# A six-layer local-attention stack on one Trainium2 core: who writes the attention mask and the rotation tables, and in which order gates, mix and projections stand

## The reference

```python
def local_attention(q, k, v):          # windows of 32 queries look at 64 keys
    ...
    mask = (it < jb) | (it > jb + w) | (jb == -1)
    sim = jnp.einsum('bhwie,bhwje->bhwij', bq, bk2) * QK_SCALE
    sim = jnp.where(mask, -jnp.finfo(sim.dtype).max, sim)
    attn = jax.nn.softmax(sim, -1)
    return jnp.einsum('bhwij,bhwje->bhwie', attn, bv2).reshape(b, h, n, d)
def attn_layer(x, Wqkv, qs, ksc, Wo):
    q, k, v = ...                      # x @ Wqkv, split in heads
    q, k = l2norm(q) * qs, l2norm(k) * ksc
    q = q * cos * scale + rotate_half(q) * sin * scale
    k = k * cos * inv + rotate_half(k) * sin * inv
    return local_attention(q, k, v) @ Wo   # heads joined
def ffn_layer(x, g, bln, W1, b1, W2, b2):
    a, gate = jnp.split((layernorm(x) * g + bln) @ W1 + b1, 2, -1)
    return a * jax.nn.gelu(gate, approximate=False) @ W2 + b2
for i in range(6):
    x = attn_layer(shift_tokens(x), ...) + x
    x = ffn_layer(shift_tokens(x), ...) + x
```

## Time and profile before

| | us |
|---|---|
| median of 3 runs | 1973.81 |
| lowest and highest | 1972.79, 1976.53 |
| profiled execution, its own time | 1982.47 |
| its span, first to last instruction | 1980.7 |
| stack, first projection to last down product | 568.7 to 1513.1 |

### The profile page before, as it was taken

One profiled execution on the slowest core, in us unless ns is written; L12 is line 12 of the kernel. 1 busy time (PEld: TensorE's weight loads), 2 busy tenths in 40 slices (PEclk: granted clock), 3 DMA queues, 4 the chain that ended last, 5 costly groups with the idle time before them and its releaser, 6 DMA issues.

```text
span 1980.7 us, 42335 instructions
## 1 busy us (share of the span) xinstructions
PE 1643.8 (83%) x17341; PEld 1101.0 (56%) x17341; DVE 1277.5 (64%) x2385; ACT 923.0 (47%) x1681; POOL 750.6 (38%) x1058
## 2 busy tenths in 40 slices
PE   3005576998778899899998999899987999999999
PEld 1002354675545556656655656656654677667576
DVE  6847674213857787878877878788863666666311
ACT  1034132332334556556655656556553666666232
POOL 0000030100256666656765756656740333334000
PEclk6556797899879999999999999999998999999999
DMA  3000002010043433423423433342321000000111
GB/s 106 20 4 0 3 1 61 22 33 14 1 129 95 132 82 91 128 73 100 134 77 88 126 97 98 97 105 84 89 54 43 1 1 2 1 1 1 33 33 32
DMA packets 73806, 113.38 MB, mean 57 GB/s; under 512 B 16086, under 2 KB 36156, under 8 KB 73582
## 3 DMA queue, kind: packets, MB, share of 16 engines
q1 hardware_dynamic: 72798, 110.43, 20.1%
q10 hardware_dynamic: 816, 0.24, 0.1%
HBM read 83.98 MB, written 27.50 MB: 56 GB/s over the span
## 4 chain that ended last, share of the span: by engine, by line
PE 60%; DVE 27%; ACT 6%; issue 5%; DMA 1%; DVEq 1%; POOL 0%; ACTq 0%; POOLq 0%; SPq 0%
PE PS L1387 8%; PE PS L1115 6%; PE PS L1106 6%; PE PS L1576 4%; PE PS L2066 4%; PE PS L2020 3%; PE PS L2045 3%; PE PS L1624 3%; PE PS L1490 3%; DVE st_t L1430 2%; DVE st_ss L1435 2%; DVE st_r L1422 2%; PE PS L1516 2%; DVE al_hist L459 1%; PE PS L1600 1%
## 5 line engine op out<-in xcount | busy, mean ns | idle before, releaser
L1463 POOL TENSOR_TENSOR st_r<-st_r,st_t 128x512 f32<-128x512 f32 x192 | 243.6, 1274 | 261.2 <-DVE st_t L1430 261.2
L1387 PE MATMUL PS<-st_wqkv,st_xs 128*128 128x512 f32 x576 | 304.1, 612 | 16.3 <-DVE st_xs L1637 9.3
L2151 POOL TENSOR_SCALAR la_p<-la_p,la_rden 128x589 f32<-128x589 f32 x64 | 112.8, 1763 | 246.0 <-DVE la_rden L2170 246.0
L1478 POOL TENSOR_TENSOR st_r<-st_r,st_gy 128x512 f32<-128x512 f32 x192 | 196.6, 1056 | 3.8
L1422 DVE TENSOR_TENSOR st_r<-PS,st_rot 128x512 f32<-128x512 f32 x192 | 129.9, 677 | 90.3 <-ACT st_sqh L1406 89.9
L2164 DVE TENSOR_REDUCE la_nmx<-PS 128x1 f32<-128x589 f32 x128 | 92.7, 766 | 91.8 <-PE PS L2028 91.8
L2126 ACT ACTIVATE la_p<-PS,la_nmx 128x589 f32<-128x589 f32 x128 | 95.1, 748 | 106.5 <-DVE la_nmx L2164 106.5
L1174 ACT ACTIVATE m_h<-PS 128x512 f32<-128x512 f32 x128 | 76.4, 598 | 142.3 <-PE PS L1106 142.3
L1406 ACT ACTIVATE st_sqh<-PS 128x512 f32<-128x512 f32 x192 | 114.3, 595 | 58.9 <-PE PS L1387 58.9
L1199 DVE SCALAR_TENSOR_TENSOR m_y<-PS,m_g,m_y 128x128 f32<-128x128 f32 x112 | 31.5, 344 | 161.0 <-PE PS L1115 161.0
L1430 DVE TENSOR_TENSOR st_t<-PS,st_rot 128x512 f32<-128x512 f32 x192 | 130.6, 680 | 0.0
(11 more groups left out here) (312 smaller groups left out, 3491.0 us busy)
## 6 DMA issues: line engine op xcount, KB each, us to landing
st_v_out<-st_v SPq DMA_DIRECT2D x48, 512.0 KB, 2.6
st_vv<-st_v_out SPq DMA_DIRECT2D x96, 256.0 KB, 3.8
st_vv<-st_v_out SPq DMA_DIRECT2D x96, 192.0 KB, 4.7
st_wqkv<-in_st_wqkv SPq DMA_DIRECT2D x18, 512.0 KB, 5.8
m_w<-in_m_w SPq DMA_DIRECT2D x32, 256.0 KB, 3.1
st_vv<-st_v_out SPq DMA_DIRECT2D x72, 64.0 KB, 1.9
st_wo<-in_st_wo SPq DMA_DIRECT2D x6, 512.0 KB
st_w<-in_st_w SPq DMA_DIRECT2D x6, 341.0 KB
```

The source lines that it names most:

```text
L1387: pe.matmul(PS[:, 2 + m % 2, :], self.xs[:, b, P * t:P * t + P], self.wqkv[:, l % 2, k, 512 * half:512 * half + 512], start=True, stop=Tru ...
L1463: pool.tensor_tensor(r, r, self.t2[:, c % 2, :], ALU.add).then_inc(self.added, 1)
L1478: pool.tensor_tensor(r, r, y[:, 8 * c:8 * c + 8].unsqueeze(2).broadcast_to([P, 8, D2]), ALU.mult)\
L2151: pool.tensor_scalar(self.p[:, v % 2, 0, :], self.p[:, v % 2, 0, :], self.rden[:, v % 4, 0:1], None, ALU.mult).then_inc(self.scaled0, 1)
```

## The change

Five things change, all in `Stack`.

1. The mask is written into banks 0 and 1 by a ScalarE copy (`act_mask`), at the end of the step before the one that uses it, once `on_ready` tells that the banks are free. The identity matmuls and `identb` are gone. The scores add onto what ScalarE wrote; for this two matmuls at T = -1 write both banks once, and `pe_mix` starts an accumulation only with the first of the four heads that share a bank and column group.
2. The rotation tables are made on GpSimd (`pool_tables`), Q's behind the second addition of the layer's last tile and K's behind its scalings, one signal each.
3. In `pe`, projection 0 of T+2 and the first half of the output transposes stand ahead of the scores; where T+2 begins a new batch half (t = 2), projection 0 stays behind the scores. At t = 1 the mix stands ahead of up product 1.
4. In `dve`, at t = 1 gate 0 stands ahead of the denominator and gate 1 behind the output; at t = 2 the down sum and the shift stand ahead of the guess, which is a function of its own.
5. In `act`, the table load for Exp stands behind the mask and not ahead of the K evacuations.

```diff
@@ dve_proj, dve_tables
-            if c == 0 and T % (B * self.TILES) == 0:
-                self.dve_tables(dve, l)
+            if c % 2 == 0 and T % (B * self.TILES) == 0:
+                dve.wait_ge(self.rot_ready, 2 * l + 1 + k)
...
+        def pool_tables(self, pool, l, k):
+            pool.wait_ge(self.qks_in, l * 16 + 16)
+            for j in range(2):
+                ins = pool.tensor_tensor(self.rot[:, k, j, :, :], self.base[:, k, j, :, :],
+                                         self.qks[:, k, j, :].unsqueeze(1).broadcast_to([P, 4, D2]), ALU.mult)
             ins.then_inc(self.rot_ready, 1)
@@ pool_proj
                 pool.tensor_tensor(r, r, self.t2[:, c % 2, :], ALU.add).then_inc(self.added, 1)
+                if c == 1 and following:
+                    self.pool_tables(pool, following, 0)
...
+            if following:
+                self.pool_tables(pool, following, 1)
@@ pe_scores
-            if T > 0:
-                pe.wait_ge(self.on_ready, T)
-            for e in range(2):
-                pe.matmul(PS[:, e, :], self.identb[:, :],
-                          self.wmask[:, min(t, 1), :].unsqueeze(1).broadcast_to([P, 8, 2 * WIN]),
-                          start=True, stop=False, skip_group_check=True)
+            pe.wait_ge(self.masked, T + 2)
...
+        def act_mask(self, act, T):
+            t = T % self.TILES
+            if T == 0:
+                act.wait_ge(self.c_in, 32)
+                act.wait_ge(self.masked, 1)
+            else:
+                act.wait_ge(self.on_ready, T)
+            act.activation(PS[:, 0:2, :].rearrange("p e (c k) -> p (e c) k", c=8),
+                           self.wmask[:, min(t, 1), :].unsqueeze(1).broadcast_to([P, 16, 2 * WIN]), ACT.Copy)\
+               .then_inc(self.masked, 1)
@@ pe_mix
-                                   self.vv[:, 4 * (T % 2) + w, :, D2 * c:D2 * c + D2], start=True, stop=True,
+                                   self.vv[:, 4 * (T % 2) + w, :, D2 * c:D2 * c + D2], start=(c % 4 == 0), stop=(c % 4 == 3),
@@ pe
+                if T == -1:
+                    for e in range(2):
+                        mm = pe.matmul(PS[:, e, :], const("centre"), self.xs[:, 0, :], start=True, stop=True)
+                    mm.then_inc(self.masked, 1)
+                if past:
+                    self.pe_turn_o(pe, T - 1, 0)
+                fresh = lead and (T + 2) % self.TILES == 0
+                if lead and not fresh:
+                    self.pe_proj(pe, T + 2, 0)
                 if here:
                     self.pe_scores(pe, T)
-                if past:
-                    self.pe_turn_o(pe, T - 1, 0)
-                if lead:
+                if fresh:
                     self.pe_proj(pe, T + 2, 0)
```

More of the change, by code:

```diff
@@ L1829, in act @@
                     self.act_gelu(act, end_of, 2)
-                if norm_of is not None or end_of is not None:
-                    self.act_table(act, ACT.Exp)
                 if turn:
@@ L1888, in pool @@
                 pool.wait_ge(self.set_up, k + 1)
+            pool.wait_ge(self.c_in, 32)
+            for k in range(2):
+                self.pool_tables(pool, 0, k)
             for T in range(self.N):
```

53 lines of the change are left out of this document (25 added, 28 removed).

## The result

| | us |
|---|---|
| changed kernel, median of 4 runs | 1955.32 |
| lowest and highest | 1947.39, 1962.84 |
| kernel before, 4 runs beside it | 1975.17 (1972.79 to 1984.96) |
| ratio, 95% interval | 0.9874 (0.9839 to 0.9908) |
| profiled execution after, its own time | 1947.39 (before 1982.47) |

The time is inside the range and the change is faster, its interval clear of 1, but by 19.9 us between these medians (25 us by the ratio) where 40.1 was forecast; the forecast ratio of 0.980 lies outside the interval. The two profiled executions differ by 35.1 us: that of before stands above its median, that of after is the fastest of its four.

A forecast was written before the change was run, and what follows sets the result against it. TensorE, 83% busy, was taken as the main bound, with a 14.75 us VectorE loop from t = 2 to 3. Gains of 27.0, 1.5, 2.4 and 9.5 less 0.3 made 40.1 us: 1973.8 to 1933.7, range 1917 to 1958.

The forecast's parts named there:

- the gate rival: At t = 1 up product 2 gets no earlier than today, 10 x 1.53 + 1.5 lost: 1950 us; chance 0.17.
- the pauses for instructions: TensorE's waits for late instructions in the stack: left at zero, 12 us either way; off by more, chance 0.07.
- Part 1, the mask: ScalarE mask, 1.06 us: t=3, 0 and 1 gain 0.53, wait 0.46 anew, about 0.07 left; wait hidden at t=2.
- Part 2, t = 1: From VectorE's first rotation product C, down product starts at C+11.0, not C+12.53: gain 1.53 us, new wait 0.9.
- Part 3, t = 2: Down sum ahead of the guess: projection 0 starts 4.6 us behind the down product, against 5.79; gain 1.17.
- Part 4: VectorE's first rotation products: t=2 to 3 stays 14.75 us; t=3 to 0 goes from 15.14 to 14.9, gain 0.2.
- Part 5, the tables: Rotation tables on GpSimd, 0.5 to 1.06 us per product, hidden; saves 9.5 us over 5 layers.
- The sum: Stack gains 27.0, 1.5, 2.4 and tables 9.5, less 0.3 for priming matmuls: 40.1 us in total.
- The steps named as unlucky: Steps whose score block starts at place 160 to 220 of 256 TensorE instructions, expected to stall; about as many as now.
- More than twelve stalls for issue: Sign that the forecast is wrong: over twelve TensorE waits for late instructions in the profile after; nine were counted before.
- The clock rival: New TensorE waits of 0.46 and 0.9 us lower its clock in 44 steps, 75 us come back: 2009; chance 0.07.

The follow-up runs named there:

- the unchanged copy: The changed kernel as it is, run again beside three kernels with added waits: 1958.96 us, ratio to before 0.9887.
- 149 waits each: Satisfied TensorE waits, 149 at the stack's start plus some per group, added to the changed kernel (1944.17 us) and the kernel before (1971.60 us).
- waits placed anew: Satisfied TensorE waits moved to an early pause (138, 135) and re-chosen per group, in the changed kernel (1927.51 us) and the kernel before (1955.34 us).

## Why the prediction was right or wrong

**Direction and range were right, the forecast time was 21.6 us too low** (1933.7 against 1955.32). Of that, 1.1 us is in the steps, 7.6 in the pauses and 11.5 between the stack of the profiles and the medians; 1.4 is the median of the kernel before, which a fourth run raised from 1973.8 to 1975.17. The range owes its upper end to the gate rival with more stalls. The gate rival did not come true, so that 1955 lies inside is in part luck. The step that failed is the pauses for instructions, left at zero. Of the chain of numbers:

- *Part 1, the mask.* Its row is 1.02 us (1080.75) where 1.06 was taken. The Trainium skill (ScalarE: Activation LUTs, "Step-by-step: what each stage is for") says that ScalarE writes PSUM faster than SBUF; the trace agrees weakly, 1.02 us against 1.05 for ScalarE's exp of the same size into SBUF (1070.73), but function and source type differ too, so the port alone was not measured. The wait for it is 0.40 us at t = 1, forecast 0.46. At t = 3 and t = 0 there is none. There the step failed: it forgot that projection 0, moved ahead of the scores, has a releaser of its own, VectorE's second product (0.40 at 1081.06). That wait stands ahead of the projection, and behind the projection the mask is ready. The size is the same, so the step came out. The worth of the part was put too low, though. Undone alone the mask costs 0.91 us a group, of which 0.43 at t = 2, where the text spoke only of the new wait, as hidden.
- *Part 2, t = 1.* From C = 1052.20 the down product starts at C+11.05 (1063.25); forecast C+11.0. The new wait is 0.63, forecast 0.9, and gone is the one before up product 1 (1055.82). Undone: 1.56 us; forecast 1.53.
- *Part 3, t = 2.* Projection 0 starts 4.52 us behind the down product (1063.25 to 1067.77); forecast 4.6. But the 1.17 us were credited to the sum's order alone. Undoing this costs 0.65 to 0.79 us and the mask's matmuls 0.43 at t = 2, together 1.1 to 1.2: the sum was right, its parts were not.
- *Part 4.* VectorE's first products stand 14.80 us apart from t = 2 to 3 (1227.05 to 1241.85; forecast 14.75) and 14.95 from t = 3 to 0 (forecast 14.9).
- *Part 5, the tables.* 0.73 us each on GpSimd, inside 0.5 to 1.06, hidden as forecast: steps with tables take 15.82, the others 15.76, where they took 17.23 and 15.54. With the 0.2 us of the step behind that is 1.84 us in each of 5 layers, 9.2 in all; forecast 9.5. Undone in the new order the tables cost more, 16 us.
- *The sum.* 40.1 forecast for the stack; 38.1 measured between the two kernels nearly without pauses. Summing the undisturbed steps of both gives 851.3 - 812.3 = 39.0.
- *The pauses*, the term left at zero with 12 us either way. The stack takes 884.1 - 851.3 = 32.8 us above its undisturbed steps before, 852.7 - 812.3 = 40.4 after, so 7.6 us of the gain went there, inside the 12. The steps named as unlucky (1, 2, 3, 14, 15, 16, 28, 41) all but 16 were; steps 4, 13, 17, 27, 29 and 40 came on top, thirteen pauses where the text had counted nine. "More than twelve stalls for issue" stood among its signs of being wrong, and this one came true. The count named places 160 to 220; the pauses of the changed kernel come in steps at places 161 to 240. The place stood in for the time between two crossings and the landing of the packet between them; both could have been read from the trace of before, crossing by crossing.
- *The clock rival* can be dropped. The waits of 0.40 and 0.63 stand in steps of granted clock 1.00, and so does the 1.26 us with projection 0 late (steps 8 and 11 of that kernel). In the changed kernel it fell, to 0.84 to 0.94, only in steps with a pause for issue (4.16, 2.86, 1.82, 2.31, 2.99 and 3.96 us in steps 2, 3, 13, 15, 27 and 29), and not in every step with a pause (2.87, 2.65 and 3.53 us in steps 1, 4 and 28 left it at 1.00). The Trainium skill (TensorE: Matmul & The Clock Gate, "A second HAM failure mode: psum-queue depth-cycling") describes a clock that swings with short idle stretches at PSUM hand-overs; at these waits the trace shows none.

**From the stack to the medians.** The forecast of 1933.7 is the median of 3 runs, 1973.8, less 40.1. In three later series the same kernel had medians of 1984.18, 1986.03 and 1986.79, so the level of a series moves by up to 13 us, and only differences within one are worth comparing. The part behind the stack, which the change does not touch, took between 500.4 and 512.2 us in 14 profiles, going with its granted clock (0.982 and 0.958 at these ends; 502.9 at 0.977 in the one of before), so single executions scatter by such amounts. Even so the medians gained less than the stacks in all four pairs: 19.9 against 31.4 us (before and after), 25.2 against 32.2 (the unchanged copy, 1984.18 to 1958.96), 27.4 against 31.1 (149 waits each), 27.8 against 38.1 (waits placed anew). For the last pair the profiles account for it: in the changed kernel the first score block came 4.0 us later (596.8 against 592.8), the part behind the stack was 0.4 us shorter (508.1 against 508.5), and the two profiled executions stand 4.4 us below and 2.2 us above their medians. The changed kernel as it is had its first score block at 592.4 and 596.2 in its two profiles, so the 4.0 us can be scatter too. Whether the other executions have longer pauses than the profiled one stays open.

## What to carry to other kernels

Count TensorE's instructions between the crossings of 256 and look how long each stretch lasts: a block of 128 small matmuls uses 256 instructions in 1.5 us, and where a stretch took less than 7 us here the next one could come late. Where the trace has the instruction queue's packets, compare their landings with the crossings: that tells which pauses are of this kind. A change that shifts instructions shifts these pauses, so measure it again with satisfied waits that move them, before its worth is judged; the waits cost next to nothing behind projections (up to 11 in a place) and in idle stretches, and 0.11 us each where nothing lies beside them. And a matmul group moved to a new position brings along the wait for its own bank: list the releasers of the moved work, not only those of the work it passes.

## What was not expected of the hardware

- With no other changes than satisfied waits on TensorE the changed kernel went from 1958.96 to 1927.51 us (ratios to before 0.9887 and 0.9709).
- The same four VectorE products of 128x256 took 1.43, 3.17 and 4.57 us: with GpSimd idle, partly beside its scalings in the kernel before, and wholly beside them in the new order (1140.94).
- TensorE never passed the crossing of 256 instructions sooner than 1.19 us after the landing of the packet that it needs, in 1408 crossings of 14 traces.
- A 128x32 operation of VectorE takes 0.76 us directly behind the reduce whose result it reads (768.82), and 0.18 when the down sum and two copies stand between (1067.70).
